# A graph transformer layer on one core: attention rounds of up to 8 slots in 3 buffers in place of 6 in 4, the base projection moved into the rounds, two VectorE operands in PSUM, and a reordered tail

## The chip, the cores and the metric

The kernel runs on 1 core of one Trainium2 chip. The metric is device time in microseconds (us), as the median of several runs. A profile is one execution of the program; its span runs from the first to the last instruction.

## The reference, cut to what matters

1250 nodes with 1024 features each, 40000 edges. A layer norm feeds a graph attention (GNN) and a linear attention; both are added to `x`, and a quantized feed-forward block follows.

```python
xn = layernorm(x)
# GNN: down-projection to 256, 4 heads of 64
xl = (h @ Wl).reshape(n, 4, 64); xr = (h @ Wr).reshape(n, 4, 64)
msg = xl[src] + xr[dst]
e = einsum('ehd,hd->eh', where(msg > 0, msg, 0.2 * msg), att)
p = exp(e - segment_max(e, dst)[dst])
out = segment_sum(p / denom[dst] * xl[src], dst) @ W_up
# linear attention: no softmax, so the 1024 x 1024 products can be taken first
q, k, v = xn @ Wq.T + bq, xn @ Wk.T + bk, xn @ Wv.T + bv
mix = (q @ k.T * SCALE) @ v @ Wo.T + bo
x = x + out + mix
# feed-forward: both operands fake-quantized in blocks of 16 (fp4 values, fp8 block scales)
gate, up = nvfp4_linear(layernorm(x), gate_w), nvfp4_linear(layernorm(x), up_w)
x = x + nvfp4_linear(silu(gate) * up, down_w)
```

## The kernel before, in words

The nodes are sorted by degree and cut into 10 chunks of 128 (`C = 10`). The kernel has three stages.

**The opening** (up to about 280 us) normalizes `x`, makes `xl` and `xr`, writes `xl` with its per-head linear term to a table in HBM (`msg_table`, rows of 264 floats), sorts the nodes, and quantizes the feed-forward weights.

**The rounds** (about 281 to 922 us) are the graph attention. Chunk `c` has room for `CAPS[c]` edges per node (54, 41, 38, 36, 34, 33, 32, 30, 28, 26: 352 slots in all). `rounds()` cuts each chunk's slots into rounds of at most `R = 6`, 62 rounds in all. A slot is one neighbour of each of the chunk's 128 nodes, fetched by one indirect DMA that GpSimd (POOL) issues: 128 rows of `msg_table` into `xg[g % 4][:, j, :]`. For round `g` with `n` slots:

- POOL first runs `rescale(g - 3)`, which multiplies the sum so far of an earlier round by its new factor and puts it in slot `n` of that round's buffer. It waits for `sum_done` of `g - 3`, so for the end of `close(g - 4)`, the last reader of the buffer that the next gathers write. Then it issues the `n` gathers, then `complete(g - 1)`, which adds the receivers' linear term to round `g - 1` (and, on a chunk's first round, prepares `beside`).
- VectorE (DVE), in the loop over `g`: copies out the matrix products that are due in this round (`take`), multiplies by `att` (scalar_tensor_tensor), sums per head (tensor_reduce), waits for `complete(g)`, adds the linear term, takes the maximum, then `add_receiver(g + 1)`, which waits for every gather of round `g + 1`, then `close(g - 1)`, a sum over the slots of round `g - 1` and its rescaled predecessor.
- ScalarE (ACT): takes its due products, then four exponentials, then `4 * n` multiplications of 66 columns in place in `xg`.

In program order DVE does:

```python
for g, (c, _, slots, first, _) in enumerate(ROUNDS):
    ...
    if g < LAST:
        step(add_receiver(g + 1))
    if g >= 1:
        close(g - 1)
```

Beside the rounds TensorE (PE) makes the 1024 x 1024 products of the linear attention, in groups of 8 matmuls into one of 4 PSUM banks (`group`): gram, p, kv, t1, t2, 16 groups each, and two bias groups. Group `n` waits until group `n - 4` is copied out. A planner written by hand (`PRODUCTS_AT`, `ROUND_0_AT = 286`, `ROUND_STEP = 10`) says in which round each group is copied out. It only orders the work; it doesn't delay a round.

**The tail** goes through the 10 chunks: `base_product(c)` (two half rows of 8 matmuls, fp32, `xhat_t` by `mat_a`), `up(c)` (the GNN's up-projection into the same banks), `residual(c)` on DVE (adds `base`, layer norm statistics), `invert_deviation` on POOL, `normalize` on ACT, `tail_scales` on DVE (block maxima and scales of this chunk's rows and of an earlier chunk's hidden values), `by_block` on POOL, `rows_rounded` and `hidden_rounded` on DVE, and then `gate_up`, `down` on PE and `finish` on DVE. The base products of chunks 0 and 1 already run beside the rounds.

Of the kernel before, what the change touches and what calls it, by code (L numbers as in the profile page):

```python
# [32 lines left out]
R = 6  # L33
# [19 lines left out]
ROUND_0_AT, ROUND_STEP = 286.0, 10.0  # L53
# [8 lines left out]
         "t2": [(4 * h + m, n) for n in range(2) for h in range(2) for m in range(4)]}  # L62
# [22 lines left out]
GATHERED = [sum(ROUNDS[i][2] for i in range(g % 4, g + 1, 4)) for g in range(LAST + 1)]  # L85


def product_groups():


    g = []
    for n in range(5):
        g += [("hid", 2 * n, "act"), ("hid", 2 * n + 1, "act")]
    g += [("lr", c, "act") for c in range(C)] + [("lin", 0, "act")]
    for kind, eng in (("gram", "act"), ("p", "dve"), ("kv", "dve"), ("t1", "act"), ("t2", "act")):
        for i in range(16):
            if kind == "t2" and i == 8:
                g += [("bias", 0, "dve"), ("bias", 1, "dve")]
            if kind == "p" and i == P0_AT:
                g.append(("p0", 0, "dve"))  # L100
            g.append((kind, i, eng))
    return g


def gps_layer(nc, x, src, dst, rms_w, w_down, wl, wr, att, w_up, wq, bq, wk_t, bk, wv_t, bv,
# [9 lines left out]
    with ExitStack() as ctx:  # L115
# [6 lines left out]
        def sem(name):  # L122
# [28 lines left out]
        round_mem = sb("round_mem", [P, 4 * (R + 1) * ROW + SLOTS * H + R * HID])  # L151
        xg = [round_mem[0:NC, i * (R + 1) * ROW:(i + 1) * (R + 1) * ROW].rearrange("p (j f) -> p j f", j=R + 1)
              for i in range(4)]
        m0 = 4 * (R + 1) * ROW
# [68 lines left out]
        xg_in = [sem(f"xg_in{i}") for i in range(4)]  # L223
# [14 lines left out]
        sort_dve, over_tick = sem("sort_dve"), sem("over_tick")  # L238
        over_edge, over_near, over_idx, over_xg, over_z, over_e, over_dve = (
# [39 lines left out]
               for i in range(2)]  # L279
        gnn_tr = xr_sb[:, :, :].rearrange("p c f -> p (c f)")[:, 0:2 * NP].rearrange("p (k n) -> p k n", k=2)  # L280
# [5 lines left out]
        gnn_out = [xr_sb[:, c, 0:HID] for c in range(C)]  # L286
        gnn_nat = [acc_sb[:, c, 0:HID] for c in range(C)]
# [15 lines left out]
        digit_f = xg_mem[0:EP, 4160:4160 + TC].bitcast(BF16).rearrange("p (a t) -> p a t", a=2)  # L303
# [75 lines left out]
        def _(sp):  # L379
# [78 lines left out]
            sp.wait_ge(acc_full, len(groups))  # L458
# [14 lines left out]
        def _(pool):  # L473
# [145 lines left out]
            def complete(g):  # L619

                c, j0, n, first, _ = ROUNDS[g]
                if first:
                    if g >= 1:
                        pool.wait_ge(lin_done, g)
                    cap = CAPS[c]
                    step(nc.gpsimd.tensor_scalar(beside[:, 0:cap, :], unused[:, c, 0:cap].unsqueeze(2).to_broadcast([NC, cap, H]), FAR, None, ALU.mult))
                    step(nc.gpsimd.tensor_tensor(beside[:, 0:cap, :], beside[:, 0:cap, :],
                                                 xr_sb[:, c, DH:H * MR:MR].unsqueeze(1).to_broadcast([NC, cap, H]), ALU.add))
                pool.wait_ge(xg_in[g % 4], 16 * GATHERED[g])
                lin = xg[g % 4][:, 0:n, DH:ROW:HR]  # L630
                nc.gpsimd.tensor_tensor(lin, lin, beside[:, j0:j0 + n, :], ALU.add).then_inc(lin_done, 1)
# [14 lines left out]
            def rescale(g):  # L646

                c, _, n, _, _ = ROUNDS[g]
                if g >= 1:
                    pool.wait_ge(sum_done, g)  # L650
                pool.wait_ge(e_done, g + 1)
                nc.gpsimd.tensor_tensor(xg[g % 4][:, n, :].rearrange("p (h d) -> p h d", d=HR),  # L652
                                        acc_sb[:, c, :].rearrange("p (h d) -> p h d", d=HR),
                                        pz[:, g % 2, n, :].unsqueeze(2).to_broadcast([NC, H, HR]), ALU.mult).then_inc(rescaled, 1)

            for g, (c, j0, n, _, _) in enumerate(ROUNDS):
                if g == 1:
                    pool.wait_ge(wq_tp, 12)
                if g >= 3:
                    rescale(g - 3)  # L660
                for j in range(n):
                    pool.indirect_dma_start(xg[g % 4][:, j, :], None, msg_table,  # L662
                                            bass.IndirectOffsetOnAxis(idx[:, c, j0 + j:j0 + j + 1], 0)).then_inc(xg_in[g % 4], 16)
                if g >= 1:
                    complete(g - 1)
                if g - 5 in LAST_OF:
                    send_attention(LAST_OF.index(g - 5))
            complete(LAST)
            for g in range(LAST - 2, LAST + 1):
                rescale(g)  # L670
# [7 lines left out]
            for k in range(-1, C + 1):  # L678
                c = k + 1
                if 1 <= c < C:  # L680
                    invert_deviation(c)
# [3 lines left out]
                if c < C:  # L685
                    pool.wait_ge(tail_scaled, k + 2)
                    by_block(ln2[c % 2], tail_factors[k % 2][1][:, 0:D // QB], D).then_inc(q_spread, 1)
                if 0 <= k - 1 < C:
# [8 lines left out]
        def _(pe):  # L697
# [156 lines left out]
            for i in range(16):  # L854
                if i in (0, 8):
                    pe.wait_ge(acc_taken["act"], taken[index_of["t1", 11 if i == 0 else 15]])
                if i == 8:

                    for h in range(2):
                        group("bias", h, [(lambda a: a, bq_col[:, k:k + 1].to_broadcast([P, P]), mat_b[:, k, h * HALF:(h + 1) * HALF],  # L860
                                           k == 0, k == KB - 1) for k in range(KB)])
# [6 lines left out]
            def base_half(c, h):  # L868

                to = acc[0:NC, base_bank(c) + h, :]  # L870
                for k in range(KB):
                    nc.tensor.matmul(to, xhat_t[:, k, c * NC:(c + 1) * NC], mat_a[:, k, h * HALF:(h + 1) * HALF],  # L872
                                     start=(k == 0), stop=False)

            def base_product(c):
                pe.wait_ge(x2_done, 1 if c == 2 else c)
                for h in range(2):
                    base_half(c, h)

            def up(c):  # L880

                pe.wait_ge(gt_taken, c + 1)
                for h in range(2):
                    for k in range(2):
                        mm = nc.tensor.matmul(acc[0:NC, base_bank(c) + h, :], gnn_tr[:, k, c * NC:(c + 1) * NC],  # L885
                                              wup_sb[:, k, h * HALF:(h + 1) * HALF], start=False, stop=(k == 1))
                mm.then_inc(x2_full, 1)

            assert len(groups) % 4 == 0
            for c, h, i in ((0, 0, 12), (1, 0, 14), (0, 1, 15), (1, 1, 15)):  # L890
                pe.wait_ge(acc_taken["act"], taken[index_of["t2", i]])
                base_half(c, h)
# [71 lines left out]
        for n in range(index_of["p", 0], len(groups)):  # L964
# [8 lines left out]
            round_of[n] = max(0, math.ceil((at - ROUND_0_AT) / ROUND_STEP))  # L973
            freed[n] = max(at, ROUND_0_AT + round_of[n] * ROUND_STEP) + 1.5
# [7 lines left out]
        def _(act):  # L982
# [23 lines left out]
            def take(n):  # L1006
# [27 lines left out]
                elif kind == "t1":  # L1034
                    h, m = ORDER["t1"][i]
                    nc.scalar.copy(mat_b[:, m, h * HALF:(h + 1) * HALF], a).then_inc(t, 1)  # L1036
                elif kind == "t2":
# [43 lines left out]
            for g, (c, _, slots, _, _) in enumerate(ROUNDS):  # L1081
# [3 lines left out]
                act.wait_ge(z_done, g + 1)  # L1085
                for h in range(H):
# [4 lines left out]
                for j in range(slots):  # L1091
                    for h in range(H):
                        cols = slice(h * HR, (h + 1) * HR)
                        ins = nc.scalar.activation(xg[g % 4][:, j, cols], xg[g % 4][:, j, cols], ACT.Copy, scale=pz[:, g % 2, j, h:h + 1])  # L1094
# [6 lines left out]
            for k in range(-1, C + 1):  # L1101
                if 1 <= k + 1 < C:
                    normalize(k + 1)
                c = k
                if 0 <= c < C:
# [3 lines left out]
                    nc.scalar.activation(silu[c % 2], acc[0:NC, 2, :], ACT.Silu, scale=cscale[0:NC, 0:1]).then_inc(silu_done, 1)  # L1109
                c = k - 1  # L1110
# [13 lines left out]
        def _(dve):  # L1124
# [273 lines left out]
            def add_receiver(g):  # L1398

                c, _, n, _, _ = ROUNDS[g]  # L1400
                dve.wait_ge(xg_in[g % 4], 16 * GATHERED[g])
                return nc.vector.tensor_tensor(m4[:, 0:n], xg[g % 4][:, 0:n, :].rearrange("p j (h d) -> p j h d", d=HR)[:, :, :, 0:DH],  # L1402
                                               xr_sb[:, c, :].rearrange("p (h d) -> p h d", d=MR)[:, :, 0:DH].unsqueeze(1)
                                               .to_broadcast([NC, n, H, DH]), ALU.add)

            def close(g):
# [4 lines left out]
                nc.vector.tensor_reduce(acc_sb[:, c, :], xg[g % 4][:, 0:n + 1, :].rearrange("p j f -> p f j"), AX.X, ALU.add).then_inc(sum_done, 1)  # L1411
# [121 lines left out]
            for g, (c, _, slots, first, _) in enumerate(ROUNDS):  # L1533
# [5 lines left out]
                step(nc.vector.scalar_tensor_tensor(m_flat[:, 0:slots], m_flat[:, 0:slots], 0.0, att_b[:, 0:slots], ALU.max, ALU.mult))  # L1539
                step(nc.vector.tensor_reduce(zz[:, 0:slots, :], m4[:, 0:slots], AX.X, ALU.add))  # L1540
                dve.wait_ge(lin_done, g + 1)
                step(nc.vector.tensor_tensor(zz[:, 0:slots, :], zz[:, 0:slots, :], xg[g % 4][:, 0:slots, DH:ROW:HR], ALU.add))
# [14 lines left out]
            tail_scales(-1)  # L1557
            residual(1)
            rows_rounded(0)

            for k in range(C + 2):
                if 1 <= k and k + 1 < C:
                    residual(k + 1)
                if k <= C:
                    tail_scales(k)
                if 0 <= k - 2 < C:
# [30 lines left out]
```

## Time and profile before

| | us |
|---|---|
| median of 3 runs | 1196.97 (1192.83 to 1197.31) |
| the profiled execution, its own time | 1195.34 |
| its span | 1193.6 |
| VectorE busy | 975.5 (82%) |
| TensorE busy | 931.1 (78%) |
| GpSimd busy | 737.9 (62%) |
| ScalarE busy | 514.2 (43%) |

The busy shares are means over three stages with different limits, so they say little by themselves. The table of slices shows the mean granted TensorE clock as well: 0.9 or 1.0 nearly everywhere, 0.5 while TensorE has nothing to do at the end of the rounds.

### The profile page before, as it was taken

What the parts mean: (1) busy time and instruction counts of PE and PEld (TensorE: products, weight loads), DVE (VectorE), ACT (ScalarE), POOL (GpSimd) and SP (SyncE); (2) the same over time, 40 slices, a digit from 0 to 9 for tenths busy, and PEclk for the clock granted to TensorE, in tenths of its full rate; (3) what the DMA queues carried; (4) which work ended last, traced back from release to release, by engine and by line L of the source; (5) the groups of instructions that cost most, each with busy time, mean ns of one, the idle gap of its engine ahead of it and who ended that gap; (6) DMA issues with size and microseconds to landing.
All of it is one profiled execution on the core that took longest, in us unless ns stands there. A gap on an engine that the chain in (4) does not pass through costs nothing.

```text
span 1193.6 us, 10168 instructions
## 1 busy us (share of the span) xinstructions
PE 931.1 (78%) x2948; PEld 453.1 (38%) x2958; DVE 975.5 (82%) x1078; ACT 514.2 (43%) x1870; POOL 737.9 (62%) x657
## 2 busy tenths in 40 slices
PE   1799999999999988899898999640000859999964
PEld 0675544444844433334343444210000424444421
DVE  6989477675999999897888898798896567887886
ACT  0123123203666666676667766665664121111111
POOL 2223438447888888888888888888884424433332
PEclk9899999999699999999999999875555879999997
DMA  7104052325244224432442222922220100000001
GB/s 240 71 2 112 11 176 63 99 76 154 77 152 144 82 73 153 147 91 73 144 147 78 77 74 79 365 80 76 80 73 30 57 1 18 18 18 18 19 35 49
DMA packets 59461, 105.29 MB, mean 88 GB/s; under 512 B 24631, under 2 KB 32468, under 8 KB 59130
## 3 DMA queue, kind: packets, MB, share of 16 engines
q0 software_dynamic: 18560, 50.70, 15.1%
q1 hardware_dynamic: 40842, 53.92, 13.4%
q8 instruction: 23, 0.38, 0.1%
q14 instruction: 36, 0.29, 0.1%
HBM read 92.30 MB, written 12.45 MB: 88 GB/s over the span
## 4 chain that ended last, share of the span: by engine, by line
DVE 29%; POOL 27%; PE 21%; issue 14%; DMA 4%; SPq 2%; ACT 2%; POOLq 0%; DVEq 0%; ACTq 0%
POOL round_mem L662 20%; PE acc L872 9%; DVE acc_sb L1411 4%; DVE round_mem L1402 3%; DVE z L1540 3%; DVE round_mem L1539 3%; PE acc L711 3%; PE acc L885 3%; PE acc L924 2%; DMA round_mem<-msg_table,idx 2%; POOL round_mem L652 2%; PE tp L942 1%; DVE round_mem L1283 1%; DVE round_mem L1157 1%; DVE round_mem L1160 1%
## 5 line engine op out<-in xcount | busy, mean ns | idle before, releaser
L662 POOL DMA_INDIRECT round_mem<-msg_table,idx x352 | 440.1, 1250 | 99.5 <-issue 91.9
L1094 ACT ACTIVATE round_mem<-round_mem,pz 128x66 f32<-128x66 f32 x1408 | 345.1, 335 | 2.0
L711 PE MATMUL acc<-wslot,big_a 128*128 128x512 f32 x512 | 228.6, 607 | 9.8 <-ACT big_b L1036 7.5
L1411 DVE TENSOR_REDUCE acc_sb<-round_mem 128x264 f32<-128x1848 f32 (+1 forms) x62 | 205.5, 3314 | 6.6 <-ACT round_mem L1094 3.9
L486 POOL TENSOR_TENSOR round_mem<-round_mem 128x1024 bf16<-128x1024 bf16 (+3 forms) x52 | 85.6, 1652 | 180.2 <-DVE round_mem L1161 92.5
L1087 ACT ACTIVATE pz<-z 128x7 f32<-128x7 f32 (+1 forms) x248 | 55.5, 296 | 229.9 <-DVE z L1547 229.9
L872 PE MATMUL acc<-big_a,xhat_t 128*128 128x512 f32 x320 | 144.6, 611 | 9.6 <-ACT big_a L1039 9.6
L711 PEld LDWEIGHTS acc<-wslot,big_a 128*128 128x128 f32 x512 | 98.8, 195 | 135.6 <-issue 121.6
L1402 DVE TENSOR_TENSOR round_mem<-round_mem,xr_sb 128x1536 f32<-128x1536 f32 (+1 forms) x62 | 104.1, 1679 | 52.9 <-DMA round_mem<-msg_table,idx 30.9
L711 PE MATMUL acc<-big_b,wslot 128*128 128x512 f32 x256 | 114.1, 606 | 5.8 <-ACT big_a L1039 4.8
L711 PE MATMUL acc<-wslot,big_b 128*128 128x512 f32 x256 | 111.2, 594 | 7.8 <-DVE big_a L1360 7.6
L900 PE MATMUL tp<-ident,acc_sb 128*128 128x128 f32 x20 | 3.9, 321 | 140.8 <-DMA acc_sb<-gnn_dram 140.2
L1539 DVE SCALAR_TENSOR_TENSOR round_mem<-round_mem,att_sb 128x1536 f32<-128x1536 f32 (+1 forms) x62 | 105.7, 1705 | 0.0
L711 PE MATMUL acc<-big_b 128*128 128x512 f32 x240 | 105.5, 599 | 0.0
L1540 DVE TENSOR_REDUCE z<-round_mem 128x24 f32<-128x1536 f32 (+1 forms) x62 | 103.4, 1667 | 2.1
L872 PEld LDWEIGHTS acc<-big_a,xhat_t 128*128 128x128 f32 x320 | 62.2, 197 | 86.3 <-issue 75.9
L711 PEld LDWEIGHTS acc<-big_b,wslot 128*128 128x128 f32 x256 | 49.3, 194 | 70.3 <-issue 62.9
L711 PEld LDWEIGHTS acc<-wslot,big_b 128*128 128x128 f32 x256 | 48.2, 190 | 70.8 <-issue 57.9
L1109 ACT ACTIVATE round_mem<-acc,cscale 128x512 f32<-128x512 f32 x10 | 6.9, 687 | 139.5 <-PE acc L924 139.5
L711 PEld LDWEIGHTS acc<-big_b 128*128 128x128 f32 x240 | 45.7, 193 | 55.2 <-issue 55.2
L900 PEld LDWEIGHTS tp<-ident,acc_sb 128*128 128x128 f32 x20 | 2.4, 156 | 143.1 <-DMA acc_sb<-gnn_dram 141.0
L652 POOL TENSOR_TENSOR round_mem<-acc_sb,pz 128x264 f32<-128x264 f32 x62 | 50.0, 806 | 10.2 <-DVE acc_sb L1411 8.8
(190 smaller groups left out, 1139.1 us busy)
## 6 DMA issues: line engine op xcount, KB each, us to landing
big_b<-in_x SPq DMA_DIRECT2D x18, 512.0 KB, 14.4
round_mem<-msg_table,idx POOLq DMA_INDIRECT x352, 2.8
out_x<-big_b SPq DMA_DIRECT2D x9, 512.0 KB
wslot<-in_wv_t SPq DMA_DIRECT2D x2, 2048.0 KB, 10.1
wslot<-in_wk_t SPq DMA_DIRECT2D x2, 2048.0 KB, 8.5
wslot<-in_wo_t SPq DMA_DIRECT2D x2, 2048.0 KB, 9.7
wslot<-in_wq SPq DMA_DIRECT2D x2, 2048.0 KB, 9.1
wslot<-in_gate_w SPq DMA_DIRECT2D x1, 2048.0 KB, 10.2
```

The lines of the kernel that those rows point to most:

```text
L486: return nc.gpsimd.tensor_tensor(v, v, factor.unsqueeze(2).to_broadcast([to.shape[0], nb, QB]), ALU.mult)
L652: nc.gpsimd.tensor_tensor(xg[g % 4][:, n, :].rearrange("p (h d) -> p h d", d=HR), acc_sb[:, c, :].rearrange("p (h d) -> p h d", d=HR), pz[ ...
L662: pool.indirect_dma_start(xg[g % 4][:, j, :], None, msg_table, bass.IndirectOffsetOnAxis(idx[:, c, j0 + j:j0 + j + 1], 0)).then_inc(xg_in[ ...
L711: mm = nc.tensor.matmul(o(acc[:, n % 4, :]), a, b, start=first, stop=last)
L872: nc.tensor.matmul(to, xhat_t[:, k, c * NC:(c + 1) * NC], mat_a[:, k, h * HALF:(h + 1) * HALF], start=(k == 0), stop=False)
L885: mm = nc.tensor.matmul(acc[0:NC, base_bank(c) + h, :], gnn_tr[:, k, c * NC:(c + 1) * NC], wup_sb[:, k, h * HALF:(h + 1) * HALF], start=Fa ...
L1087: ins = nc.scalar.activation(pz[:, g % 2, 0:slots + 1, h], z[:, g % 3, 0:slots + 1, h], ACT.Exp, scale=-1.0, bias=z[:, (g + 1) % 3, top_sl ...
L1094: ins = nc.scalar.activation(xg[g % 4][:, j, cols], xg[g % 4][:, j, cols], ACT.Copy, scale=pz[:, g % 2, j, h:h + 1])
L1402: return nc.vector.tensor_tensor(m4[:, 0:n], xg[g % 4][:, 0:n, :].rearrange("p j (h d) -> p j h d", d=HR)[:, :, :, 0:DH], xr_sb[:, c, :].r ...
L1411: nc.vector.tensor_reduce(acc_sb[:, c, :], xg[g % 4][:, 0:n + 1, :].rearrange("p j f -> p f j"), AX.X, ALU.add).then_inc(sum_done, 1)
L1539: step(nc.vector.scalar_tensor_tensor(m_flat[:, 0:slots], m_flat[:, 0:slots], 0.0, att_b[:, 0:slots], ALU.max, ALU.mult))
L1540: step(nc.vector.tensor_reduce(zz[:, 0:slots, :], m4[:, 0:slots], AX.X, ALU.add))
```

## The change

- `R = 8`, `BUFFERS = 3`: 49 rounds of up to 8 slots (7 + 6 + 5 + 5 + 5 + 5 + 4 + 4 + 4 + 4); the 352 slots stay. Round `g` gathers into `xg[g % 3]`. POOL runs `rescale(g - 2)` ahead of the gathers of round `g`.
- The receivers' values and `att`, which DVE reads in `add_receiver` and in the scalar_tensor_tensor, are copied by ACT into free PSUM (`show_receivers`, `att_ps`), and DVE reads them there.
- All 20 half rows of the base projection become groups (`base`) beside the rounds, after t2 and the two bias groups; ACT copies each into `xhat_t`. In the tail, `up(c)` brings a half row back into PSUM with one fp32 matmul by the identity, and goes on with the up-projection.
- In the tail DVE does `residual(k + 2)` behind `tail_scales(k)`, where it did `residual(k + 1)` ahead of it; `normalize` and `invert_deviation` move with it.
- The planner's constants become `ROUND_0_AT = 288`, `ROUND_STEP = 12.1`. Some scratch tiles of the opening move.

```diff
-R = 6
+R = 8
+BUFFERS = 3
-ROUND_0_AT, ROUND_STEP = 286.0, 10.0
+ROUND_0_AT, ROUND_STEP = 288.0, 12.1
...
-            if kind == "t2" and i == 8:
-                g += [("bias", 0, "dve"), ("bias", 1, "dve")]
...
+    g += [("bias", 0, "dve"), ("bias", 1, "dve")] + [("base", i, "act") for i in range(2 * C)]
...
             for g, (c, j0, n, _, _) in enumerate(ROUNDS):
                 if g == 1:
                     pool.wait_ge(wq_tp, 12)
-                if g >= 3:
-                    rescale(g - 3)
+                if g >= 2:
+                    rescale(g - 2)
                 for j in range(n):
-                    pool.indirect_dma_start(xg[g % 4][:, j, :], None, msg_table,
+                    pool.indirect_dma_start(xg[g % BUFFERS][:, j, :], None, msg_table,
...
             def up(c):
 
+                if c == 0:
+                    pe.wait_ge(acc_taken["act"], count["act"])
+                elif c >= 2:
+                    pe.wait_ge(x2_done, 1 if c == 2 else c)
                 pe.wait_ge(gt_taken, c + 1)
                 for h in range(2):
+                    to = acc[0:NC, base_bank(c) + h, :]
+                    nc.tensor.matmul(to, ident[:], base_at[c][:, 4 * h:4 * h + 4, :], start=True, stop=False)
...
+            def show_receivers(c):
+
+                nc.scalar.copy(xr_ps[c].rearrange("p (h d) -> p h d", d=DH),
+                               xr_sb[:, c, :].rearrange("p (h d) -> p h d", d=MR)[:, :, 0:DH]).then_inc(xr_ps_done, 1)
...
             def add_receiver(g):
 
-                dve.wait_ge(xg_in[g % 4], 16 * GATHERED[g])
+                dve.wait_ge(xg_in[g % BUFFERS], 16 * GATHERED[g])
...
-                                               xr_sb[:, c, :].rearrange("p (h d) -> p h d", d=MR)[:, :, 0:DH].unsqueeze(1)
+                                               xr_ps[c].rearrange("p (h d) -> p h d", d=DH).unsqueeze(1)
...
             residual(0)
-            tail_scales(-1)
-            residual(1)
-            rows_rounded(0)
-
-            for k in range(C + 2):
-                if 1 <= k and k + 1 < C:
-                    residual(k + 1)
+            for k in range(-1, C + 2):
                 if k <= C:
                     tail_scales(k)
+                if k + 2 < C:
+                    residual(k + 2)
```

## Rows read from the trace of the kernel before

**Rows 1.** Windows: the rounds, their end, four stretches of the tail, one tail period

```profile
core 0: us, PE busy (x) PEld busy (x) DVE busy (x) ACT busy (x) POOL busy (x), PEclk, DMA share, GB/s
284.28:907.12 622.84, 471.02 (x1136) 217.31 (x1134) 559.73 (x433) 408.89 (x1660) 519.04 (x485) 0.87 0.36 111
907.12:922.59 15.47, 0.00 (x0) 0.00 (x0) 11.08 (x10) 6.77 (x28) 2.70 (x2) 0.50 0.00 0
...
935.22:996.76 61.54, 47.44 (x135) 21.74 (x136) 44.56 (x76) 10.10 (x15) 21.82 (x17) 0.89 0.02 7
...
1047.21:1071.49 24.28, 23.20 (x77) 10.59 (x76) 20.60 (x31) 3.31 (x4) 9.80 (x7) 1.00 0.06 22
1142.43:1193.60 51.17, 24.37 (x109) 10.31 (x110) 34.71 (x67) 7.45 (x10) 13.20 (x11) 0.80 0.10 39
```

**Rows 2.** Instruction groups by shape, 300 to 900 us: DVE, then POOL

```profile
L1411 DVE TENSOR_REDUCE acc_sb<-round_mem 128x264 f32<-128x1848 f32 x41 | 142.2, 3469 | 1.4
...
L1402 DVE TENSOR_TENSOR round_mem<-round_mem,xr_sb 128x1536 f32<-128x1536 f32 x38 | 67.1, 1766 | 24.9 <-DMA round_mem<-msg_table,idx 24.3
L1411 DVE TENSOR_REDUCE acc_sb<-round_mem 128x264 f32<-128x1584 f32 x18 | 53.9, 2993 | 0.6
...
L1402 DVE TENSOR_TENSOR round_mem<-round_mem,xr_sb 128x1280 f32<-128x1280 f32 x20 | 29.9, 1495 | 6.0 <-DMA round_mem<-msg_table,idx 5.5 <-DVE z L1547 0.2
...
L662 POOL DMA_INDIRECT round_mem<-msg_table,idx x329 | 414.5, 1260 | 91.7 <-issue 86.0 <-ACT pz L1087 5.0
```

**Rows 3.** Timeline of part of one round (start, us, engine, line)

```profile
561.60 0.95 POOL L662 DMA_INDIRECT round_mem<-msg_table,idx  x1 [0.30 <-issue]
...
562.77 0.63 POOL L652 TENSOR_TENSOR round_mem<-acc_sb,pz 128x264 f32<-128x264 f32 x1
...
563.55 0.98 POOL L662 DMA_INDIRECT round_mem<-msg_table,idx  x1 [0.16 <-issue]
...
564.51 1.76 DVE L1402 TENSOR_TENSOR round_mem<-round_mem,xr_sb 128x1536 f32<-128x1536 f32 x1 [0.80 <-DMA round_mem<-msg_table,idx]
564.67 5.88 ACT L1094 ACTIVATE round_mem<-round_mem,pz 128x66 f32<-128x66 f32 x24
...
569.66 1.75 DVE L1539 SCALAR_TENSOR_TENSOR round_mem<-round_mem,att_sb 128x1536 f32<-128x1536 f32 x1
569.88 2.35 POOL L662 DMA_INDIRECT round_mem<-msg_table,idx  x1 [0.30 <-issue]
```

**Rows 4.** Timeline: a DVE instruction with an operand in PSUM, and POOL beside it

```profile
402.53 0.73 DVE L1360 SCALAR_TENSOR_TENSOR big_a<-big_b,p_sb,acc 128x512 f32<-128x512 f32 x1
...
402.74 0.96 POOL L662 DMA_INDIRECT round_mem<-msg_table,idx  x1 [0.30 <-issue]
```

**Rows 5.** Timeline from the last rounds to the tail's first product

```profile
904.25 2.97 DVE L1411 TENSOR_REDUCE acc_sb<-round_mem 128x264 f32<-128x1584 f32 x1 [0.62 <-POOL round_mem L652]
...
907.29 2.07 POOL L652 TENSOR_TENSOR round_mem<-acc_sb,pz 128x264 f32<-128x264 f32 x1 [3.18 <-DVE acc_sb L1411]
...
918.01 3.43 DVE L1411 TENSOR_REDUCE acc_sb<-round_mem 128x264 f32<-128x1848 f32 x1 [3.87 <-ACT round_mem L1094]
...
929.25 5.93 PE L885 MATMUL acc<-wslot,xr_sb 128*128 128x512 f32 x8
```

**Rows 6.** The chain that ended last: transfers on it, and products in one tail period

```profile
330.73 6.09 DMA round_mem<-msg_table,idx
...
1052.33 13.79 PE acc L872 x32
1066.12 3.43 PE acc L885 x8
```

**Rows 7.** Timeline of the tail, DVE: a wait; L1159 lengthened, and alone

```profile
1054.55 1.22 DVE L1164 TENSOR_REDUCE round_mem<-round_mem 128x64 f32<-128x1024 f32 x1 [2.92 <-ACT round_mem L987]
...
1066.60 3.25 DVE L1159 SCALAR_TENSOR_TENSOR round_mem<-round_mem 128x1024 f32<-128x1024 f32 x1
...
1115.15 1.22 DVE L1159 SCALAR_TENSOR_TENSOR round_mem<-round_mem 128x1024 f32<-128x1024 f32 x1
```

More of the change, by code:

```diff
@@ L61 @@
 ORDER = {"p": FROM_HIGH, "kv": FROM_LOW, "t1": FROM_LOW,
-         "t2": [(4 * h + m, n) for n in range(2) for h in range(2) for m in range(4)]}
+         "t2": [(4 * h + m, n) for n in range(2) for h in range(2) for m in range(4)],
+         "base": [(c, h) for c in range(C) for h in range(2)]}
 TURNED_AFTER = {("lin", 0): 2, ("gram", 2): 3, ("gram", 6): 4, ("gram", 7): 5, ("gram", 8): 6, ("gram", 10): 7,
@@ L84 @@
 LAST_OF = [g for g, (_, _, _, _, last) in enumerate(ROUNDS) if last]
-GATHERED = [sum(ROUNDS[i][2] for i in range(g % 4, g + 1, 4)) for g in range(LAST + 1)]
+GATHERED = [sum(ROUNDS[i][2] for i in range(g % BUFFERS, g + 1, BUFFERS)) for g in range(LAST + 1)]
 def product_groups():
@@ L222, in gps_layer @@
         neigh_in = sem("neigh_in")
-        xg_in = [sem(f"xg_in{i}") for i in range(4)]
+        xg_in = [sem(f"xg_in{i}") for i in range(BUFFERS)]
         pool_const = sem("pool_const")
@@ L286, in gps_layer @@
         gnn_out = [xr_sb[:, c, 0:HID] for c in range(C)]
+        xr_ps = [tp[0:NC, c % 2, 0:HID] for c in range(C)]
+        att_ps = tpb[0:NC, 0, 0:2 * HID].bitcast(F32)
         gnn_nat = [acc_sb[:, c, 0:HID] for c in range(C)]
@@ L668, in _ @@
             complete(LAST)
-            for g in range(LAST - 2, LAST + 1):
+            for g in range(LAST - 1, LAST + 1):
                 rescale(g)
@@ L856, in _ @@
                     pe.wait_ge(acc_taken["act"], taken[index_of["t1", 11 if i == 0 else 15]])
[L857 to L861, printed above, removed]
                 halves_in("t2", i, 9)
@@ L973, in gps_layer @@
             round_of[n] = max(0, math.ceil((at - ROUND_0_AT) / ROUND_STEP))
+            if kind == "base" and ORDER["base"][i][1] == 1:
+                round_of[index_of["base", ORDER["base"].index((ORDER["base"][i][0], 0))]] = round_of[n]
             freed[n] = max(at, ROUND_0_AT + round_of[n] * ROUND_STEP) + 1.5
@@ L1079, in _ @@
                 act.wait_ge(over_done, 1)
-            for g, (c, _, slots, _, _) in enumerate(ROUNDS):
+            def show_receivers(c):
+                nc.scalar.copy(xr_ps[c].rearrange("p (h d) -> p h d", d=DH),
+                               xr_sb[:, c, :].rearrange("p (h d) -> p h d", d=MR)[:, :, 0:DH]).then_inc(xr_ps_done, 1)
+            act.wait_ge(xr_in, 16 * C)
+            show_receivers(0)
+            show_receivers(1)
+            act.wait_ge(wq_taken, 12)
+            nc.scalar.copy(att_ps.rearrange("p (h d) -> p h d", d=DH), att_sb[0:NC]).then_inc(xr_ps_done, 1)
+            for g, (c, _, slots, first, _) in enumerate(ROUNDS):
                 for n in due("act", g):
@@ L1085, in _ @@
                 act.wait_ge(z_done, g + 1)
+                if first and 1 <= c < C - 1:
+                    show_receivers(c + 1)
                 for h in range(H):
@@ L1109, in _ @@
                     nc.scalar.activation(silu[c % 2], acc[0:NC, 2, :], ACT.Silu, scale=cscale[0:NC, 0:1]).then_inc(silu_done, 1)
+                if k + 2 < C:
+                    normalize(k + 2)
                 c = k - 1
```

77 lines of the change are left out of this document (39 added, 38 removed).

## The prediction

> **What bounds the kernel now.** I read the windows by stage first, because the busy shares of the whole span mix three stages. The rounds fill 622.8 us between the first and the last scalar_tensor_tensor [rows 1]: 61 steps, 10.2 us each. DVE is busy 559.7 us of them and POOL 519.0. POOL's sequencer adds a pause of 0.30 us ahead of each gather [rows 3] (91.7 us in all [rows 2]), which makes POOL occupied for about 610 of the 622.8 us. So the rounds run at POOL's pace: 5.68 slots x 1.25 us, and then what lengthens a gather. The groups by shape show that: 329 gathers take 414.5 us, 1260 ns each [rows 2], while an undisturbed one takes 0.95 [rows 3]. The excess, 102 us or 1.7 us a round, comes from gathers that begin while DVE runs L1402 or L1539, two instructions with both inputs in SBUF: L1539 runs from 569.66 to 571.41, and the gather that begins at 569.88 takes 2.35 us and ends 0.8 behind it [rows 3]. In the tail I read one period: 24.28 us, PE busy 23.20, DVE 20.60 [rows 1]. PE is the bound: base product 13.79, up-projection 3.43 in eight recorded passes [rows 6], the rest gate, up, down and transposes. DVE is next, with 2.92 us of waiting for `normalize` [rows 7].
>
> **The change in the rounds: what the third buffer does to the order.** This decides the forecast. Ahead of the gathers of round g POOL waits for `close(g - 3)`, because that round's buffer is the one to be filled. In DVE's order `close(g - 3)` stands at the end of iteration g - 2, and `add_receiver(g)`, which needs all gathers of round g, stands in the middle of iteration g - 1, ahead of `close(g - 2)`. With four buffers the gathers had one iteration more. Now each link depends on the last: end of close(g-3), rescale, all gathers of round g, landing, add_receiver(g), close(g-2). What DVE can do meanwhile (the multiply by `att`, a reduce, the maximum, the copies of products) lies under the gathers; the gathers themselves lie under nothing. One link, with a mean of 352/49 = 7.18 slots:
>
> - close to rescale 0.07 [rows 5]; rescale 0.63; to the first gather 0.15 [rows 3].
> - 7.18 gathers at 0.95 + 0.30 us, less the last pause: 8.68. I take the undisturbed length: L1402 is over before the gathers begin, L1539 now has an operand in PSUM, and beside a DVE instruction with a PSUM operand a gather took 0.96 us [rows 4]. If L1539 should still hold POOL, one gather a round is longer by up to 1.4 (2.35 against 0.95); both ends are kept.
> - end of the last gather (562.55) to add_receiver (564.51): 1.96 [rows 3].
> - add_receiver: 1766 ns for 6 slots, 1495 for 5 [rows 2], so 0.271 a slot: 2.09. The operand in PSUM is costed at nothing: the 512 columns of L1360 with one took 0.73 us [rows 4], about a third of the 1536 of L1402 with its fixed part.
> - a gap of 0.03, then close: 3469 ns for 6 slots, 2993 for 5 [rows 2], 0.476 a slot: 4.03.
>
> Sum: 0.07 + 0.63 + 0.15 + 8.68 + 1.96 + 2.09 + 0.03 + 4.03 = **17.6 us a round**, of which DVE waits some 6. Rounds 3 to 48 go through it, 46 links, 810 us. `complete(g-1)`, behind the gathers, and the maximum end within the 1.96 us; on a chunk's first round the two instructions ahead of it make them some 0.4 late, 4 us in all.
>
> Ahead of the links: POOL issues rounds 0 and 1 as before, then `rescale(0)` waits for the first exponentials: first multiply at 284.3 [rows 1], 4.7 for it, the reduce and the maximum, 0.9 for the exponentials and some 1.3 for the rescale, so round 2 is gathered from about 291 on. Eight gathers (9.7), landing (1.96), add_receiver (2.3) and the first close (3.9) end at about 309. Behind them: multiply, reduce and maximum of the last round 4.7, exponentials and 28 multiplications at 0.245 us [rows 3] 7.8, last close 3.9: 16. So 309 + 810 + 4 + 16 = 1139.
>
> A landing that the other transfers of the core delay is now always on the path. The trace has such a wait of 6.09 us on its chain [rows 6] against 1.96 to 2.9; six loads of weights of 2 MB, and then the tail's weights and `x`, fall into the rounds. A load hits a landing about every other time, and the long stretch hits two or three: 5 x 3 + a few = 20 us as an estimate, between 0 and 50. The rounds then end at **1159**, where they ended at 921.4 [rows 5] (918.01 + 3.43): 238 later.
>
> ACT does 28.7 multiplications at 0.245 and 4 exponentials, about 8 us, and up to two copies of products in 17.6: no bound. The 20 new copies are hidden there. PE needs 14 us for two groups in such a round: hidden too, and if its cover were gone (clock at half) two groups would need 28. The planner counts with 12.1 us a round, so products are ready early rather than late.
>
> **The tail.** The planner's arithmetic (7.3 us a group from 240 on) puts base groups 14 to 19 behind the last round. Four of them can run during the last rounds, as there are four banks; the last two start once ACT is done with its multiplications, about 4 us ahead of the last close, and cost 2 x 6.9 (half of 13.79 each [rows 6]) and some 2 for a clock at half (0.50 there [rows 1]). Then transposes. `up(0)` starts 14.6 us behind the last close, not 7.9 (929.25 less 921.4 [rows 5]).
>
> In the period, 13.79 of PE go; the two identity matmuls are four recorded passes at 0.43, so 1.7 come. PE needs 24.3 - 13.8 + 1.7 = 12.2, and DVE becomes the bound. Its wait of 2.92 [rows 7] goes, as `residual(k + 2)` and `normalize` are now a period ahead. Its busy 20.60 holds some 4.5 us of instructions lengthened beside POOL (3.25 for L1159 [rows 7], 1.22 where it is alone); of these about 2 should go because POOL's spreads now lie under the residual, which has a PSUM operand. With gaps of about 0.8 that gives 19.7; I take 20, between 17 (no lengthening) and 24.3 (a PE at half clock).
>
> Residual(0) to residual(3) took 61.5 [rows 1], with two base products; by DVE's own work it is 37 now. Six periods: 120 for 145.7. From residual(9) to the last store 51.2 [rows 1]; it is earlier in its period now, so 57. Tail from residual(0): 214. `up(0)` itself is 5.2 with the identity passes at full clock, 5.93 before [rows 5].
>
> Sum: 1159 + 14.6 + 5.3 + 214 = **1393 span**. The profiled execution lies 1.7 above its span and the median of the runs 1.6 above that: I say **1395**, 198 more than 1197. The tail gives back some 46 less 7, the rounds cost 238.
>
> **A rule weighed.** SBUF: the trace says that a gather beside a two-input DVE instruction took 2.35 us and beside one with a PSUM operand 0.96 [rows 3, 4]. The Trainium skill, "SBUF — State Buffer", section "Summary: rules for kernel authors", says that DVE with two SBUF inputs and a reading GpSimd instruction exclude each other for a whole instruction. By it the PSUM operands take the 1.7 us a round away, and the sum stays at 1395; this trace agrees.
>
> **The rivals.**
>
> *Gathers hidden (faster).* If the gathers of a round were under DVE's work, the rounds would run at DVE's pace: multiply, reduce, add at 2.1 each, close 4.0, small ones and copies about 1.6: 11.9 us x 49 = 583 in place of 638, and with the tail's 39 the time is about 1197 - 55 - 39 = **1103**. It decides if POOL's wait is met a whole iteration before the gathers are needed. For it: POOL alone would need 10.3 us a round. Against: the order of `close` and `add_receiver` in DVE's list, which is fixed. 4%. The Trainium skill, "Trainium Kernel Development and Optimization", section "Best Practices", advises double-buffering to overlap transfers with compute; taken as enough, three buffers would do, and this rival's time would follow. No run here shows it yet.
>
> *L1539 still holds POOL.* 46 x 1.2 (between 1.0 and 1.4) more on the links: **1450**. Against it: rows 4. 5%.
>
> *PE becomes late.* With half a clock between groups it would hold up copies in rounds and stretch the tail's period to 24: 8 periods x 4, and some 10 in the rounds: **1435**. For it: PE is busy two thirds of a round, and the clock falls when it is idle (0.50 while it has no work [rows 1]). 7%.
>
> **How the numbers follow.** Forecast as told 84%, hidden gathers 4%, L1539 5%, PE 7%. The low end takes landings without delay (-20) and a tail period of 17 (-27): 1348, rounded to 1345; the high end takes in the two slow rivals: 1450. All but one case are slower by far more than 0.5%, which is what a measurement of this kernel can tell from no change: slower 0.95, same 0.01, faster 0.04.
>
> **What would show it.** In the rounds: DVE's L1402 waits about 6 us in each round, released by the gathers' DMA; POOL waits about as long for the close (L1411) ahead of each rescale; 17 to 18 us a round; gathers at 0.95 throughout; 49 closes. In the tail: no PE base product, a period near 20 with DVE busy throughout. I am wrong if rounds take near 12 us, if POOL doesn't wait for closes, or if gathers stay at 2.2 beside L1539.

## The result, and the profile after

| | before | after |
|---|---|---|
| median, us | 1197.14 (4 runs) | 1407.88 (1398.69 to 1408.97, 4 runs) |
| ratio, 95% interval | | 1.1745 (1.1681 to 1.1808) |
| span of the profiled execution | 1193.6 | 1407.0 |

The change costs 211 us. The forecast was 1395, with a range of 1345 to 1450.

The windows of the profile after, by stage (columns as in [rows 1]): the rounds, their end, the way to the tail, then in the tail residual(0) to residual(3), one period, and residual(9) to the end.

```profile
284.53:1131.30 846.77, 622.49 (x1360) 278.14 (x1358) 533.30 (x355) 404.54 (x1626) 383.63 (x458) 0.85 0.27 81
1131.30:1148.52 17.22, 4.33 (x5) 1.85 (x6) 12.62 (x10) 9.65 (x36) 2.28 (x3) 0.56 0.02 9
1148.52:1168.25 19.73, 18.58 (x46) 8.30 (x45) 0.01 (x2) 1.63 (x4) 7.93 (x4) 0.95 0.24 74
1168.25:1211.56 43.31, 27.65 (x85) 12.49 (x84) 34.70 (x66) 10.27 (x15) 21.02 (x14) 0.80 0.03 10
1235.09:1259.40 24.31, 15.99 (x49) 6.71 (x48) 18.80 (x30) 3.41 (x4) 9.79 (x7) 0.72 0.05 22
1350.59:1407.00 56.41, 28.30 (x112) 10.90 (x110) 43.06 (x78) 7.45 (x10) 15.30 (x13) 0.81 0.11 44
```

In [rows 1] DVE was busy 90% of the rounds and POOL 83%, beside its pauses. Now DVE is busy 63% and POOL 45%: nobody is full, which is what a chain of waits looks like in such a table. The page's groups say who waits for whom (busy, mean ns, idle before it, releaser); the first two answer to L662 and L1411 in [rows 2]:

```profile
L667 POOL DMA_INDIRECT round_mem<-msg_table,idx x352 | 337.4, 958 | 99.8 <-issue 95.1
...
L1429 DVE TENSOR_REDUCE acc_sb<-round_mem 128x264 f32<-128x2112 f32 (+2 forms) x49 | 198.0, 4041 | 6.0 <-ACT round_mem L1110 4.4
...
L657 POOL TENSOR_TENSOR round_mem<-acc_sb,pz 128x264 f32<-128x264 f32 x49 | 30.6, 626 | 371.9 <-DVE acc_sb L1429 363.8
L1561 DVE TENSOR_TENSOR z<-z,round_mem 128x28 f32<-128x28 f32 (+2 forms) x49 | 10.4, 211 | 260.5 <-POOL round_mem L636 245.8
...
L1420 DVE TENSOR_TENSOR round_mem<-round_mem,tp 128x1792 f32<-128x1792 f32 (+2 forms) x49 | 101.4, 2070 | 66.6 <-DMA round_mem<-msg_table,idx 46.2
```

Two waits point at each other. POOL's rescale (L657) waits 363.8 us in all for DVE's close (L1429), some 7.6 us a round; DVE waits 245.8 us for POOL's `complete` (L636), which stands behind the gathers, and 46.2 more for the gathers to land, 6.3 us a round together. A gather now takes 958 ns, not 1260. One link in the timeline of the kernel after (start, us, engine, line), from close to close:

```profile
620.36 0.63 POOL L657 TENSOR_TENSOR round_mem<-acc_sb,pz 128x264 f32<-128x264 f32 x1 [7.35 <-DVE acc_sb L1429]
...
621.14 1.03 POOL L667 DMA_INDIRECT round_mem<-msg_table,idx  x1 [0.15 <-issue]
621.19 2.01 DVE L1557 SCALAR_TENSOR_TENSOR round_mem<-round_mem,tpb 128x1792 f32<-128x1792 f32 x1
...
622.48 0.96 POOL L667 DMA_INDIRECT round_mem<-msg_table,idx  x1 [0.30 <-issue]
...
623.23 2.02 DVE L1559 TENSOR_REDUCE z<-round_mem 128x28 f32<-128x1792 f32 x1
...
628.79 0.96 POOL L667 DMA_INDIRECT round_mem<-msg_table,idx  x1 [0.30 <-issue]
...
629.77 0.27 POOL L636 TENSOR_TENSOR round_mem<-round_mem 128x28 f32<-128x28 f32 x1
...
630.14 0.21 DVE L1561 TENSOR_TENSOR z<-z,round_mem 128x28 f32<-128x28 f32 x1 [4.89 <-POOL round_mem L636]
...
631.68 2.02 DVE L1420 TENSOR_TENSOR round_mem<-round_mem,tp 128x1792 f32<-128x1792 f32 x1 [1.08 <-DMA round_mem<-msg_table,idx]
633.74 3.93 DVE L1429 TENSOR_REDUCE acc_sb<-round_mem 128x264 f32<-128x2112 f32 x1
...
637.75 0.63 POOL L657 TENSOR_TENSOR round_mem<-acc_sb,pz 128x264 f32<-128x264 f32 x1 [7.71 <-DVE acc_sb L1429]
```

Read it by who runs when. From 620.4 to 629.7 only the gathers advance; DVE does its multiply and reduce beside them and then stands. From 629.8 to 631.7 the last gather lands, and `complete` and two short instructions of DVE fit in. From 631.7 to 637.7 only DVE advances, and POOL stands until close has ended. The pattern came in all 46 links: the first close ends at 309.1 and the 47th at 1131.4, so 17.88 us each. The second gather begins while L1557 runs, and it takes 0.96 us; in [rows 3] such a gather, beside the multiply with both operands in SBUF, took 2.35.

Where the 213.4 us of span come from: the rounds end at 1147.7 and ended at 921.4, 226.2 later; from there to residual(0) 20.6 us, 13.8 before, 6.8 more; from residual(0) to the end 238.8, 258.4 before, 19.6 less.

### The profile page after: what moved, and what is told of

Same layout as the page of the kernel before. It is cut to its first block, busy times and chain, and to the rows that moved or that the text cites. A ratio compares the mean times of both kernels' runs of the same rounds, so it can differ in the third digit from the quotient of the medians.

```text
span 1407.0 us, 10110 instructions
## 1 busy us (share of the span) xinstructions
PE 1037.6 (74%) x2998; PEld 487.1 (35%) x2998; DVE 939.3 (67%) x1000; ACT 515.5 (37%) x1849; POOL 605.4 (43%) x631
## 4 chain that ended last, share of the span: by engine, by line
DVE 40%; POOL 27%; issue 12%; PE 8%; DMA 8%; SPq 2%; ACT 1%; DVEq 0%; POOLq 0%; ACTq 0%
POOL round_mem L667 20%; DVE acc_sb L1429 14%; DVE round_mem L1420 7%; DMA round_mem<-msg_table,idx 7%; PE acc L716 3%; PE acc L889 3%; DVE round_mem L1176 2%; POOL round_mem L657 2%; DVE round_mem L1175 2%; DVE round_mem L1174 2%; POOL round_mem L491 2%; DVE round_mem L1173 1%; PE acc L887 1%; DVE round_mem L1299 1%; DVE round_mem L1158 1%
## 5 line engine op out<-in xcount | busy, mean ns | idle before, releaser
L667 POOL DMA_INDIRECT round_mem<-msg_table,idx x352 | 337.4, 958 | 99.8 <-issue 95.1
L716 PE MATMUL acc<-wslot,big_a 128*128 128x512 f32 x512 | 245.8, 641 | 77.3 <-ACT big_b L1036 40.4
L1429 DVE TENSOR_REDUCE acc_sb<-round_mem 128x264 f32<-128x2112 f32 (+2 forms) x49 | 198.0, 4041 | 6.0 <-ACT round_mem L1110 4.4
L657 POOL TENSOR_TENSOR round_mem<-acc_sb,pz 128x264 f32<-128x264 f32 x49 | 30.6, 626 | 371.9 <-DVE acc_sb L1429 363.8
L1561 DVE TENSOR_TENSOR z<-z,round_mem 128x28 f32<-128x28 f32 (+2 forms) x49 | 10.4, 211 | 260.5 <-POOL round_mem L636 245.8
L1103 ACT ACTIVATE pz<-z 128x8 f32<-128x8 f32 (+2 forms) x196 | 44.3, 298 | 373.6 <-issue 190.3
L716 PE MATMUL acc<-wslot,big_b 128*128 128x512 f32 x256 | 123.7, 646 | 46.6 <-DVE big_a L1376 33.8
L1420 DVE TENSOR_TENSOR round_mem<-round_mem,tp 128x1792 f32<-128x1792 f32 (+2 forms) x49 | 101.4, 2070 | 66.6 <-DMA round_mem<-msg_table,idx 46.2
L491 POOL TENSOR_TENSOR round_mem<-round_mem 128x1024 bf16<-128x1024 bf16 (+3 forms) x52 | 85.6, 1653 | 132.7 <-DVE round_mem L1177 87.6
L1559 DVE TENSOR_REDUCE z<-round_mem 128x28 f32<-128x1792 f32 (+2 forms) x49 | 101.4, 2069 | 1.7
L1557 DVE SCALAR_TENSOR_TENSOR round_mem<-round_mem,tpb 128x1792 f32<-128x1792 f32 (+2 forms) x49 | 101.0, 2061 | 0.0
L889 PE MATMUL acc<-wslot,xr_sb 128*128 128x512 f32 x80 | 46.3, 710 | 0.0
L1497 DVE TENSOR_TENSOR big_b<-acc,big_b 128x1024 f32<-128x1024 f32 x10 | 12.2, 1223 | 49.5 <-PE acc L889 49.5
```

Of the source, the lines that this page charges most:

```text
L491: return nc.gpsimd.tensor_tensor(v, v, factor.unsqueeze(2).to_broadcast([to.shape[0], nb, QB]), ALU.mult)
L657: nc.gpsimd.tensor_tensor(xg[g % BUFFERS][:, n, :].rearrange("p (h d) -> p h d", d=HR), acc_sb[:, c, :].rearrange("p (h d) -> p h d", d=HR ...
L667: pool.indirect_dma_start(xg[g % BUFFERS][:, j, :], None, msg_table, bass.IndirectOffsetOnAxis(idx[:, c, j0 + j:j0 + j + 1], 0)).then_inc( ...
L716: mm = nc.tensor.matmul(o(acc[:, n % 4, :]), a, b, start=first, stop=last)
L889: mm = nc.tensor.matmul(to, gnn_tr[:, k, c * NC:(c + 1) * NC], wup_sb[:, k, h * HALF:(h + 1) * HALF], start=False, stop=(k == 1))
L1103: ins = nc.scalar.activation(pz[:, g % 2, 0:slots + 1, h], z[:, g % 3, 0:slots + 1, h], ACT.Exp, scale=-1.0, bias=z[:, (g + 1) % 3, top_sl ...
```

## The experiments

Ten kernels, each timed in 3 rounds against the kernel before on the same chip.

**1. The rounds as before, all else of the change kept.** The scratch tiles `digit_f` and `tri`, which only the opening uses, go back to their old places too.

```diff
-R = 8
-BUFFERS = 3
+R = 6
+BUFFERS = 4
-ROUND_0_AT, ROUND_STEP = 288.0, 12.1
+ROUND_0_AT, ROUND_STEP = 286.0, 10.0
-                if g >= 2:
-                    rescale(g - 2)
+                if g >= BUFFERS - 1:
+                    rescale(g - BUFFERS + 1)
```

> The changed kernel with rounds of 6 slots in 4 buffers again, all else of the change kept (PSUM operands, base projection in the rounds, reordered tail). Theory of the exposed gathers: DVE sets the pace of the rounds, 9.6 us each (multiply, reduce, add 1.7 each, close 3.3, small ones and copies), POOL needs 8.1; the rounds lose some 40 us against the kernel before, the tail some 13, so about 1145. Rival (the other parts of the change cost the time: operands in PSUM, more products beside the rounds): the time stays above 1300.

Measured: 1119.6 us, ratio to before 0.934 (0.932 to 0.937). The rounds take 9.4 us each, close to close. So the size of the rounds and the number of buffers together cost 288 us, and all the rest of the change gains 77. The page's groups for this kernel:

```profile
L667 POOL DMA_INDIRECT round_mem<-msg_table,idx x352 | 337.1, 958 | 99.9 <-issue 87.1
L1429 DVE TENSOR_REDUCE acc_sb<-round_mem 128x264 f32<-128x1848 f32 (+1 forms) x62 | 206.3, 3327 | 6.0 <-ACT round_mem L1110 3.8
...
L657 POOL TENSOR_TENSOR round_mem<-acc_sb,pz 128x264 f32<-128x264 f32 x62 | 38.8, 626 | 82.7 <-DVE acc_sb L1429 76.7
```

The gathers are as short as in the kernel after, and POOL's wait for the close is 76.7 us, not 363.8. That remaining wait costs little, since DVE is the bound: from the first close to the 60th (301.2 to 854.3) it is busy 537.1 us of 553.2; experiment 10 shows what is left to gain. How much of the rounds' gain comes from the PSUM operands alone wasn't run with four buffers. The expectation was 25 us too high: the rounds ended 53 us earlier than before, not 40 (9.4 us each, not 9.6), and the tail behind them took 20 less, not 13.

**2. DVE reads the receivers and `att` from SBUF again** (the copies into PSUM still run).

```diff
-                                               xr_ps[c].rearrange("p (h d) -> p h d", d=DH).unsqueeze(1)
+                                               xr_sb[:, c, :].rearrange("p (h d) -> p h d", d=MR)[:, :, 0:DH].unsqueeze(1)
-                                                    att_ps.unsqueeze(1).to_broadcast([NC, slots, HID]), ALU.max, ALU.mult))
+                                                    att_b[:, 0:slots], ALU.max, ALU.mult))
```

> The changed kernel, but DVE reads the receivers and att from SBUF again; the copies into PSUM still run. Theory: the two-input multiply holds one gather a round, which is now on the path: 46 x 1.0 to 1.4 more, about 1463; the add comes when no gather is under way and costs nothing. Rival (the hold depends on POOL's load, not on the operands): within 5 us of 1408.

Measured: 1478.1 us, 70 above the changed kernel and 15 above the expectation. The lengthening is there, and it hits two POOL instructions, not the gathers alone. Its page:

```profile
L667 POOL DMA_INDIRECT round_mem<-msg_table,idx x352 | 363.3, 1032 | 99.9 <-issue 97.7
L657 POOL TENSOR_TENSOR round_mem<-acc_sb,pz 128x264 f32<-128x264 f32 x49 | 73.4, 1499 | 370.0 <-DVE acc_sb L1429 363.8
```

Against the kernel after the gathers take 25.9 us more and the rescales 42.8: 68.7, which is all of the 68.5 by which the span grew. By its timeline each round but the first has one of the two: in 24 rounds a gather that begins 0.3 to 1.3 us into the multiply takes 2.1 us in the mean, and in 24 others the rescale, which begins less than 0.2 us into it, takes 2.4. Here the multiply ends at 798.62 and the rescale 0.48 us behind it:

```profile
796.61 2.01 DVE L1557 SCALAR_TENSOR_TENSOR round_mem<-round_mem,att_sb 128x1792 f32<-128x1792 f32 x1
796.78 2.32 POOL L657 TENSOR_TENSOR round_mem<-acc_sb,pz 128x264 f32<-128x264 f32 x1 [8.30 <-DVE acc_sb L1429]
```

**3. Three buffers, close ahead of add_receiver.** The buffers, the rounds and all work stay; two calls in DVE's list change places.

```diff
-                if g < LAST:
-                    step(add_receiver(g + 1))
                 if g >= 1:
                     close(g - 1)
+                if g < LAST:
+                    step(add_receiver(g + 1))
```

> The changed kernel, 3 buffers, but in DVE's list close(g - 1) stands ahead of add_receiver(g + 1). Theory: close(g-2) no longer needs the gathers of round g to land, only the maximum of round g-1, which needs complete(g-1) behind those gathers: 0.9 + 8.7 + 0.3 + 0.6 + 4.0 = 14.5 us a round, 155 less in all, about 1250. Rival (three buffers are too few whatever the order; or the gathers' own rate is the bound): above 1380.

Measured: 1265.4 us, 142 less than the changed kernel, 14.8 us from close to close; the expectation had 14.5 and 155 less. In the timeline the close now follows the maximum at once, and what it waits for is `complete`, which still stands behind the gathers:

```profile
612.90 0.27 POOL L636 TENSOR_TENSOR round_mem<-round_mem 128x32 f32<-128x32 f32 x1
...
613.28 0.22 DVE L1561 TENSOR_TENSOR z<-z,round_mem 128x32 f32<-128x32 f32 x1 [1.69 <-POOL round_mem L636]
...
613.78 3.95 DVE L1429 TENSOR_REDUCE acc_sb<-round_mem 128x264 f32<-128x2112 f32 x1
...
617.64 1.75 DVE L1420 TENSOR_TENSOR round_mem<-round_mem,tp 128x1536 f32<-128x1536 f32 x1
617.81 0.62 POOL L657 TENSOR_TENSOR round_mem<-acc_sb,pz 128x264 f32<-128x264 f32 x1 [4.63 <-DVE acc_sb L1429]
```

**4. As 3, and `complete` behind the second gather of the next round.**

```diff
                 for j in range(n):
+                    if g >= 1 and j == 2:
+                        complete(g - 1)
                     pool.indirect_dma_start(xg[g % BUFFERS][:, j, :], None, msg_table,
...
-                if g >= 1:
-                    complete(g - 1)
```

> As the one before, and POOL runs complete(g - 1) behind the second gather of round g, not behind the last. Theory: nothing on DVE's path stands behind the gathers of the next round; DVE sets the pace with 11.9 to 12.3 us a round, POOL needs some 11: rounds end near 885, and the time is about 1150. Rival (three buffers too few in any order): above 1250, no better than the one before.

Measured: 1141.7 us, ratio 0.954 (0.952 to 0.956), 12.1 us from close to close. Three buffers with rounds of 8 are now faster than the kernel before: 266 us lay in the place of two calls, `close` in DVE's list and `complete` in POOL's. The gathers are not wholly hidden; DVE still waits 31.7 us in all for them, as its page says:

```profile
L1420 DVE TENSOR_TENSOR round_mem<-round_mem,tp 128x1792 f32<-128x1792 f32 (+2 forms) x49 | 101.2, 2066 | 52.2 <-DMA round_mem<-msg_table,idx 31.7
```

It stays behind experiment 1 by 22 us.

**5. In the tail, `up` ahead of `turn_q`** (on the changed kernel). It came from the trace after. In the chain that ended last, in one period of the tail, PE's work stands in full:

```profile
1224.31 1.94 POOL round_mem L491
1226.25 0.05 issue
1226.30 1.03 PE tpb L913 x8
1227.33 1.81 PE acc L887 x2
1229.14 3.34 PE acc L889 x4
1232.48 0.86 PE acc L887 x2
1233.34 1.73 PE acc L889 x4
1235.07 0.02 issue
1235.09 1.24 DVE big_b L1497
```

POOL's last product of the rounded rows (L491) releases the transposes of `turn_q` (L913), and the identity and up-projection passes (L887, L889) stand behind them in PE's list, though nothing that they need comes from there. DVE's residual waits for them, 3.9 to 5.2 us in each of residual(3) to residual(8). Part of that wait is TensorE's clock: the first half row's passes take 1.81 and 3.34 us, the second's 0.86 and 1.73, so 2.6 of the 5.17 us in this period, by estimate, and 1.7 in the next, where they take 1.00 and 3.32.

```diff
-                if k != 0 and max(k, 0) + 2 < C:
-                    up(max(k, 0) + 2)
+                if k == -1:
+                    up(2)
                 if 0 <= k < C:
                     gate_up(k)
                 if 0 <= k - 1 < C:
                     down(k - 1)
+                if k >= 0 and k + 3 < C:
+                    up(k + 3)
                 if 0 <= k + 1 < C:
                     turn_q(k + 1)
```

> The changed kernel, and in TensorE's list of the tail up(k + 3) stands ahead of turn_q(k + 1), where it stood behind it. Theory: the tail's period of 24 us is a wait of the residual on up, which stands behind turn_q, and so behind the rounding of the same period; without it DVE sets 20 us, some 20 us less in all: about 1387. Rival (TensorE's half clock is the bound in the tail): within 5 us of 1408.

Measured: 1377.1 us, 31 less, where 20 were expected: the first three residuals take 38.4 us in place of 43.3, and the periods are shorter than the 20 us expected. The period is 19.46 us, and DVE is full (window of one period, columns as in [rows 1]):

```profile
1242.94:1262.40 19.46, 13.61 (x48) 5.97 (x48) 18.70 (x31) 2.80 (x4) 9.79 (x7) 0.82 0.07 28
```

TensorE's granted clock is 0.82 there and was 0.72, so it isn't at full speed in either; the edit moved only the place in the list, and with it the residual's wait for TensorE is gone, but for 0.9 us at residual(9).

**6. Rounds of 6 in 3 buffers.** `round_mem` and the buffers' distance keep the room of 8 slots.

```diff
-R = 8
+R = 6
+ROOM = 8
-ROUND_0_AT, ROUND_STEP = 288.0, 12.1
+ROUND_0_AT, ROUND_STEP = 286.0, 10.0
```

> The changed kernel with rounds of 6 slots, still in 3 buffers (62 rounds). Theory: the same chain with 5.68 slots a round is 14.7 to 14.9 us, and its fixed parts are paid 13 times more: about 1454. Rival (the larger rounds cost the time, not the third buffer): below 1408.

Measured: 1448.9 us, 14.9 us from close to close. Against experiment 1, which differs in the number of buffers and, beside it, only in the distance between them and the place of two scratch tiles, the fourth buffer is worth 329 us at 6 slots; larger rounds alone are a gain of 41 in this order.

**7 and 8. Experiments 1 and 4, each with the tail of 5.**

> Rounds of 6 slots in 4 buffers with all else of the change, and up ahead of turn_q. Theory: both gains add: 1120 less 20 is about 1100. Rival: the tail doesn't move, 1120.

> Rounds of 8 slots in 3 buffers with close and complete ahead, and up ahead of turn_q. Theory: 1142 less 20 is about 1122, behind the 4 buffers of 6 by about 20, since the wait for the gathers isn't all gone. Rival: the tail doesn't move, 1142.

Measured: 1094.0 us (ratio 0.914, 0.912 to 0.916) and 1116.3 (0.933, 0.931 to 0.935). Each gains 25 to 26, where 20 were expected; the periods of both tails are 19.5.

**9. The old order of the tail** on the changed kernel: residual(k + 1), normalize and invert_deviation ahead again, the base projection still in the rounds.

```diff
             for k in range(-1, C + 2):
+                if 1 <= k and k + 1 < C:
+                    residual(k + 1)
                 if k <= C:
                     tail_scales(k)
-                if k + 2 < C:
-                    residual(k + 2)
+                if k == -1:
+                    residual(1)
```

> The changed kernel with the tail's order of before on DVE, ACT and POOL (residual(k + 1), normalize and invert_deviation ahead), base projection still in the rounds. Theory: in the new order each residual waits for the up that stands behind turn_q (4 to 5 us of a period of 23.9); in the old order that wait is covered and the wait for normalize (2.9) is back: a period of 22 to 22.5, so the reordering by itself gave nothing: 1395 to 1408. Rival (the reordering is worth its 2.9 us a period, as predicted): 8 x 3 slower, about 1430.

Measured: 1403.3 us (1399.9 to 1406.3), the same as or a little below the changed kernel; the two were timed on different occasions, so 4.6 us is not claimed. From residual(0) to the end it takes 237.6 us (238.8 in the changed kernel). Its period is 22.3 us (the window of one, then from its timeline the wait for normalize and the L1173 that is lengthened; in the changed kernel it takes 0.42, at 1239.24):

```profile
1247.13:1269.47 22.34, 15.90 (x48) 6.74 (x48) 20.59 (x32) 3.42 (x4) 9.80 (x7) 0.75 0.06 24
1252.53 1.22 DVE L1180 TENSOR_REDUCE round_mem<-round_mem 128x64 f32<-128x1024 f32 x1 [0.99 <-ACT round_mem L987]
1258.11 2.14 DVE L1173 TENSOR_SCALAR round_mem<-round_mem 128x512 int32<-128x512 int32 x1
```

The wait for normalize is 0.8 to 1.0 us a period, and not the 2.9 that the expectation had back: this tail differs from that of the kernel before in the base projection alone, which took some 2 us of the wait with it. No residual of these periods waits for TensorE.

**10. All that helped, with 4 buffers of 6**: experiment 7, with close ahead of add_receiver and complete behind the second gather.

> Rounds of 6 slots in 4 buffers, up ahead of turn_q, and close and complete ahead too. Theory: with 4 buffers DVE is already busy through its rounds (9.4 us each, hardly a wait for gathers), so the orders that repair 3 buffers give nothing: 1094 within 6. Rival (waits for complete are still on the path): 15 or more faster.

Measured: 1088.7 us (1087.9 to 1089.3), ratio 0.9086 (0.907 to 0.910). It is the fastest version of this study, 108 us below the kernel before. The two orders give 5 us here, where they gave 266 with three buffers.

## Why the prediction was right, point by point

- **The order with the third buffer, and the link.** Right, and shown by experiments 3, 4 and 6. The sum was 17.6 us; 46 links took 822.3, 17.88 each. The gathers' own length was 958 ns, the close 3952 ns for 7 slots on the formula's 3.95, the first close ended at 309.1 (309 forecast), the tail end of the rounds took 16.3 (16). One sign was told in the wrong place: not L1402 (now L1420) waits 6 us for the gathers' DMA, but the instruction behind `complete` waits 5.3 a link and L1420 1.0. The sum of both is the 6 us told, since `complete` stands behind the same gathers; POOL's wait is 7.6.
- **Landings.** Sized too high. I added 20 us for transfers in the way and 4 for first rounds. Above the undisturbed sum of 810 there were 12, of which 8 in the landings, first rounds included (98.1 us, where 46 x 1.96 are 90.2), and 2 in the gathers. In the links L1420 waited 4.5 us once and 2.3 once; all other waits were 2.0 or less. So one landing was late by the 3 us that the forecast counted five times (the 6.09 of [rows 6] runs from the gather's start, where 2.9 is usual), and that a load meets every other landing is shown by no run. The rounds ended at 1147.7, 11 ahead of the forecast.
- **The PSUM operands free POOL.** Right. Their price if they didn't was told as 55; experiment 2 measured 70, because the lengthening also falls on the rescale, which I had left out of the rival. The traces hold a wider count than the one row that the prediction shows: in the kernel before, the gathers that begin during L1402 take 1.92 us in the mean and those during L1539 2.03 (102 in all), beside its two reductions (L1540, L1411) none takes more than 1.02; in experiment 1, 141 begin during the same add and multiply, now with an operand in PSUM, and none takes more than 1.03. The Trainium skill, "SBUF — State Buffer", section "Summary: rules for kernel authors", names any reading GpSimd instruction, so the rescale is in its rule; this trace agrees, with 1499 ns for it against 626.
- **The way to the tail.** 20.6 us, 19.9 forecast (14.6 + 5.3): two base groups (`base` 18 and 19) did run alone behind the last multiplications.
- **The tail.** Here a step failed, and its error partly hid behind the landings' in the total: 25 us too low here, 11 too high there, so the total came out 14 us of span and 13 of time off. That the two errors offset each other for 11 us is luck. "DVE becomes the bound", with a period of 20: measured 23.2, as (1350.59 - 1211.56) / 6, with DVE busy 18.80 of 24.31. From residual(0) on the tail took 238.8 and not 214: 43.3 to residual(3) in place of 37, 139.0 for the six periods in place of 120, 56.4 behind them (57). The forecast had PE's work as a sum, 12.2 us under DVE's 20, and left out its place in the list: ahead of `up(k + 2)` stands `turn_q(k + 1)`, which waits for the end of DVE's own rounding. Moving it (experiment 5) gave the period of 19.5, where the sum from DVE's rows was 19.7. The rival "PE becomes late" had the period right (24) and its reason in part: the granted clock was 0.72 in the period, and the half speed of the first half row made up 1.7 to 2.6 us of a wait of 4 to 5; but with the list in order a clock of 0.82 was enough.
- **What the reordered tail gives.** The forecast counted 2.9 us a period for the covered wait for normalize and about 2 for instructions no longer lengthened. Experiment 9 shows that the reorder alone gave nothing: it exchanged one wait for another. Together with experiment 5 the period is 19.5 in place of 22.3, of which the wait for normalize is 1.0 and DVE's busy time 1.9 (20.59 to 18.70), nearly all of it L1173; so the 2 us were right, and the 2.9 was 1.0 once the base products had gone. The old order together with the early `up` wasn't run; as no residual waits for TensorE in experiment 9's periods, little is to be expected of it.
- **The rival of hidden gathers.** It is refuted as the kernel stands. Its condition was right, its price only in part: with POOL's wait met a whole iteration earlier (experiment 4) the rounds take 12.1 us (11.9 worked out), but the time is 1141.7 and not 1103. The rounds end 41 us ahead of the kernel before, not 55, and from there on 13 us go and not 39, for the reason given at the tail; with experiment 5's tail it is 1116.3. The Trainium skill's advice to double-buffer ("Trainium Kernel Development and Optimization", section "Best Practices"), named with this rival, is to overlap transfers with compute; here three buffers didn't bring that about by their number, since a third stage, `close`, held each buffer for an iteration more.
- **A slip.** "The tail gives back some 46 less 7" is 44.4 less 6.1 by the forecast's own terms; the 1395 doesn't rest on it.

## What to carry to other kernels

Count the buffers a pipeline needs from the order of the instruction lists: from the release of a buffer, in the list of the engine that releases it, to the first instruction that needs its new content, and compare the work between the two with issue plus landing. If it is less, the whole transfer goes onto the path, round after round, and then moving the release ahead of the consumer can be worth nearly as much as a buffer (266 us here for two calls at 8 slots, 329 for the fourth buffer at 6). When an instruction is called covered, look also at what stands ahead of it in its own engine's list, and at what that waits for.

## What the runs showed of the hardware that was not expected

What POOL loses beside a DVE instruction with both operands in SBUF was costlier on a short instruction than on the gathers. With both operands of the multiply there (experiment 2), POOL's rescale of 626 ns took 1499 in the mean over 49 rounds, and 2.4 us in the 24 rounds in which it began less than 0.2 us into the multiply. A gather was hit in 24 rounds, one in each, and took 2.1 us there in place of 0.96 (1032 ns in the mean over all 352). In the changed kernel the rescale at 637.75 begins as early, 0.16 us into the multiply, and takes 0.63.
